# TensorE signals twice an expert tile instead of four times

## The chip, the cores and the metric

The kernel runs on one core of a Trainium2 chip. The metric is the device time of one execution in microseconds (us), the median over several runs.

## The reference

128 graphs of 128 nodes with 128 features go through a graph attention layer and then a mixture of experts, both with a layer norm ahead and a residual behind. The change touches the experts alone:

```python
logits = einsum('bsd,de->bse', x, gate_w) + gate_b        # 16384 tokens, 16 experts
top_probs, top_idx = top_k(softmax(logits), 2)            # two experts a token, gates normalized to 1
h1 = einsum('bsd,edh->bseh', x, w1)                       # 128 -> 256
h2 = einsum('bsd,edh->bseh', x, w2)                       # 128 -> 256
hidden = silu(h1) * h2
expert_out = einsum('bseh,eho->bseo', hidden, w3)         # 256 -> 128
out = x + einsum('bseo,bse->bso', expert_out, dispatch)
```

All data is float32.

## The kernel before

The attention part comes first, in 32 groups of four graphs. As each group's rows are ready, GpSimd scatters them into `first_list`, an array in device memory that is sorted by the token's first expert. When the list stands, the experts work through it in tiles of 256 rows (two times 128). Each tile's result is added to its rows, and GpSimd scatters these into `second_list`, sorted by the token's second expert (line 632). The second pass does the same over that list and scatters the rows to the output (line 643). A list has 72 tiles: 48 whole (one expert), 8 lone and 16 mixed (two experts, 128 rows each), so there are 144 tiles in all. `r` is the list, `j` the tile, `u` the tile's buffer of `S` = 12, and `n` the turn over these buffers. A part of each list's whole tiles runs in a loop on the engines (`Fori`), and the rest is written out.

The program has no scheduler. Each engine has a program of its own, and `done(engine, semaphores, n, u, d)` makes it wait until the step of tile `u + d` has been signalled; the semaphores of a kind stand in a list of `TURNS` = 4, taken in turn. For a tile `j` the engines do this:

- SyncE loads the rows to `xin` (lines 442 and 446) and copies the expert's first weights within the core to `we` (line 436), up to 12 tiles ahead.
- VectorE normalizes the rows, in the first list alone (line 989, named `xn`).
- TensorE, in `tile` from line 1248, does in this order: the gate product of tile j into `psG`, signal `s_G`; the up product into `psU`, signal `s_U` (both line 1258, four matmuls of 256 columns in a whole tile, and each shows as two in the profile); the two transposes of tile j + 2 into `psX` (line 1273), signal `s_xTp`; the second product of tile j - 1 into `psY` (line 1283), signal `s_Y`. A signal is an increment on the last matmul of its group.
- ScalarE, in `tile` from line 732: silu of the gate product (line 736, waits for `s_G`), then the copy of the transposed rows of tile j + 2 from `psX` to `xT` (line 741, waits for `s_xTp` and for `s_U`). The profile names `xT` and the hidden tile `hid` by the array `X` in which they lie, and the gate and up products by `psS`.
- VectorE: the product of silu and up product, `hid` (line 1083, waits for `s_U` and silu), then the normalization of a later tile, then the gated sum of tile j - 1 into `xin` (line 1092, waits for `s_Y`).
- GpSimd: every second tile it issues four scatters, two for each of the two tiles before (lines 632 and 643), when VectorE's sum is signalled.

TensorE in turn waits for `xT` and silu of two tiles before ahead of the gate product, for `hid` of two tiles before ahead of the up product, for the rows and `xn` ahead of the transposes, and for `hid` of the tile before ahead of the second product.

Of the kernel before, what the change touches and what calls it, by code (L numbers as in the profile page):

```python
# [5 lines left out]
def gnn_then_moe(nc: bass.Bass, x, adj, a0, a1, a2, a3, gate_w, gate_b, w1, w2, w3, out):  # L6
# [37 lines left out]
    S = 12  # L44
    SURE = (TOKENS - E * (W2 - 1)) // W2
    PAIRS = TOKENS // W2 - SURE
    TILES = SURE + E // 2 + PAIRS
# [31 lines left out]
    with ctx:  # L79
# [6 lines left out]
        def sem(name):  # L86
            return ctx.enter_context(nc.semaphore(name))
# [115 lines left out]
        TURNS = 4  # L203
# [9 lines left out]
        psG = [psS[:, 0, :], psS[:, 1, :]]  # L213
        psU = [psS[:, 2, :], psS[:, 3, :]]
# [72 lines left out]
        s_in = [sem(f"s_in{i}") for i in range(S)]  # L287
        s_we = [sem(f"s_we{i}") for i in range(S)]
        s_xn = [sem(f"s_xn{i}") for i in range(TURNS)]
        s_xTp = [sem(f"s_xTp{i}") for i in range(TURNS)]  # L290
        s_xT = [sem(f"s_xT{i}") for i in range(TURNS)]
        s_G = [sem(f"s_G{i}") for i in range(TURNS)]
        s_U = [sem(f"s_U{i}") for i in range(TURNS)]
        s_silu = [sem(f"s_silu{i}") for i in range(TURNS)]
        s_hid = [sem(f"s_hid{i}") for i in range(TURNS)]
        s_Y = [sem(f"s_Y{i}") for i in range(TURNS)]
# [11 lines left out]
        def wait(eng, s, value):  # L308

            if not isinstance(value, int) or value > 0:  # L310
                eng.wait_ge(s, value)
# [21 lines left out]
        LEAD, LAG = 2, 1  # L333
# [9 lines left out]
        def offsets(i, after):  # L343

            if i is None:
                return [after(S)[0] - S]
            return [k - i for k in after(i) if k < TILES]
# [19 lines left out]
        def wait_in(eng, n, u, d):  # L367

            wait(eng, s_in[(u + d) % S], (n + (u + d) // S + 1) * 32)

        def done(eng, sems, n, u, d):

            wait(eng, sems[(u + d) % TURNS], n * (S // TURNS) + (u + d) // TURNS + 1)
# [283 lines left out]
        def _(act):  # L657
# [65 lines left out]
            def closing():  # L723
                new_rows_turned(G - 2)
                new_rows_turned(G - 1)
                second_gate(G // 2 - 2)
                second_gate(G // 2 - 1)

            steps(step)
            closing()  # L730

            def tile(n, u, i, on):
                if on(0):
                    done(act, s_hid, n, u, -2)
                    done(act, s_G, n, u, 0)
                    nc.scalar.activation(silu[:, u % 2, :], psG[u % 2], ACT.Silu).then_inc(s_silu[u % TURNS], 1)  # L736
                for d in offsets(i, turned_after):
                    k = (u + d) % S
                    done(act, s_U, n, u, d - XTS)
                    done(act, s_xTp, n, u, d)  # L740
                    nc.scalar.activation(xT[:, k % XTS, :], psX[k % 2][:, 0:W2], ACT.Copy).then_inc(s_xT[k % TURNS], 1)  # L741

            def pad(r, rows, width, e):
# [359 lines left out]
        def _(pe):  # L1103
# [144 lines left out]
            def tile(r, n, u, i, weights, experts, between=None):  # L1248


                if weights:
                    done(pe, s_xT, n, u, 0)
                    parts = weights()
                    for half, out, s_out, s_free in ((0, psG[u % 2], s_G, s_silu), (1, psU[u % 2], s_U, s_hid)):
                        done(pe, s_free, n, u, -2)
                        for at, rows in parts:
                            for c in range(HC):
                                last = mm(out[:, c * W2 + rows.start:c * W2 + rows.stop],  # L1258
                                          at[:, half * H + c * P:half * H + (c + 1) * P], xT[:, u % XTS, rows],
                                          start=True, stop=True)  # L1260
                        last.then_inc(s_out[u % TURNS], 1)
                if between:
                    between()
                if experts:
                    e = experts()
                for d in offsets(i, turned_after):
                    k = (u + d) % S
                    done(pe, s_xT, n, u, d - 2)
                    if r == 0:
                        done(pe, s_xn, n, u, d)  # L1270
                    wait_in(pe, n, u, d)
                    for t in range(2):
                        last = nc.tensor.transpose(psX[k % 2][:, t * P:(t + 1) * P], xin[:, k, t, ROW:ROW2],  # L1273
                                                   ident[:, :])
                    last.then_inc(s_xTp[k % TURNS], 1)
                if experts:
                    k = (u - LAG) % S
                    done(pe, s_y, n, u, -LAG - 2)
                    done(pe, s_hid, n, u, -LAG)
                    for t in range(2):  # L1280
                        for c in range(HC):
                            at = c * W2 + t * P
                            last = mm(psY[k % 2][:, t * D:(t + 1) * D], hid[:, k % HIDS, at:at + P],  # L1283
                                      wts[:, ds(e[t] * EW + (UP + c * D), D)],
                                      start=(c == 0), stop=(c == HC - 1))
                    last.then_inc(s_Y[k % TURNS], 1)
# [47 lines left out]
```

## Time and profile before

| | us |
|---|---|
| median of 3 runs | 867.44 |
| lowest and highest | 866.37 and 876.10 |
| the profiled execution | 875.39 |
| its span, first to last instruction | 873.6 |
| mean granted TensorE clock | 0.937 |

The rows come from one profiled execution, so sums are made against 875.39. Busy time of TensorE is the union of matmuls, whose ends are modelled; PEld is the weight load of the same engine, which runs beside the matmuls. "Idle before" is the time in which the engine did nothing ahead of an instruction, with what ended it: another engine's instruction, "issue" (nothing that the profile shows) or "remote" (no instruction of this core that ended just then). In the timeline, consecutive instructions of a line are merged, with their count at the end.

### The profile page before, as it was taken

The numbers are of one execution on the slowest core, as the hardware profiler recorded it, in microseconds if no ns is written. First come the engines' busy times: TensorE is split into PE (matmuls) and PEld (weight loads), VectorE is DVE, ScalarE is ACT, GpSimd is POOL, SyncE is SP. The second block draws the span as 40 slices with busy tenths as digits, with TensorE's granted clock in tenths as the row PEclk, the third lists the DMA queues.
The fourth block names the chain that finished last, engine by engine and source line by source line (L and its number), as shares of the span: only waits on it lengthen the run. The fifth ranks groups of instructions, "written<-read, shape, count | busy, mean of one in ns | idle before, by whom it ended". The sixth has DMA issues, their size and how long they took to land.

```text
span 873.6 us, 17532 instructions
## 1 busy us (share of the span) xinstructions
PE 739.4 (85%) x4422; PEld 595.1 (68%) x4423; DVE 503.5 (58%) x1706; ACT 415.4 (48%) x1011; POOL 516.7 (59%) x670
## 2 busy tenths in 40 slices
PE   3899999999999766888988888987898888878895
PEld 2465656565666645677878777886787777777785
DVE  3799999999999863545454544543333233233332
ACT  7999999999999221222222222222222222222221
POOL 3337777778787765554645455554555645545555
PEclk9999999999999767999989988998999999999998
DMA  5233544332321144766666555634766565666640
GB/s 157 73 109 115 157 129 147 96 105 81 105 90 35 33 148 156 216 220 190 225 213 197 171 184 168 197 126 131 232 212 190 178 211 179 197 200 198 189 131 8
DMA packets 127462, 133.28 MB, mean 153 GB/s; under 512 B 16362, under 2 KB 98545, under 8 KB 127378
## 3 DMA queue, kind: packets, MB, share of 16 engines
q1 hardware_dynamic: 107008, 94.66, 36.0%
q0 software_dynamic: 15616, 34.38, 11.6%
q10 hardware_dynamic: 4754, 3.25, 1.2%
q8 instruction: 36, 0.59, 0.3%
q14 instruction: 48, 0.39, 0.2%
HBM read 52.28 MB, written 41.19 MB: 107 GB/s over the span
## 4 chain that ended last, share of the span: by engine, by line
PE 43%; DVE 23%; issue 16%; another core or an unknown queue 12%; ACT 4%; POOL 1%; DMA 0%; DVEq 0%; ACTq 0%; POOLq 0%
PE psS L1258 23%; PE bank L1283 13%; DVE stage L886 3%; PE bank L1273 3%; DVE stats L817 3%; DVE late L933 3%; DVE bestix L909 2%; DVE late L949 2%; DVE X L1083 1%; PE psS L1166 1%; ACT silu L736 1%; DVE late L968 1%; DVE best L905 1%; ACT late L689 1%
## 5 line engine op out<-in xcount | busy, mean ns | idle before, releaser
L1258 PE MATMUL psS<-X,late 128*128 128x256 f32 (+1 forms) x1280 | 264.1, 355 | 6.0 <-issue 5.8
L1258 PEld LDWEIGHTS psS<-X,late 128*128 128x128 f32 x1280 | 212.7, 203 | 26.0 <-issue 7.1
L1083 DVE TENSOR_TENSOR X<-silu,psS 128x512 f32<-128x512 f32 x144 | 98.8, 686 | 226.2 <-remote 119.8
L736 ACT ACTIVATE silu<-psS 128x512 f32<-128x512 f32 x144 | 86.0, 597 | 282.3 <-remote 147.2
L632 POOL DMA_INDIRECT second_list<-xin x144 | 142.2, 988 | 129.7 <-DVE xin L1092 88.7
L643 POOL DMA_INDIRECT out_dram<-xin x144 | 141.7, 984 | 122.4 <-DVE xin L1092 82.7
L1283 PE MATMUL bank<-wts,X 128*128 (+1 forms) x1152 | 168.1, 292 | 36.5 <-DVE X L1083 33.5
L1283 PEld LDWEIGHTS bank<-wts,X 128*128 128x128 f32 x1152 | 150.6, 203 | 45.9 <-issue 45.8
L583 POOL DMA_INDIRECT first_list<-stage,slot x128 | 128.1, 1001 | 52.6 <-issue 41.2
L1092 DVE SCALAR_TENSOR_TENSOR xin<-bank,xin 128x128 f32<-128x128 f32 x288 | 87.5, 346 | 100.7 <-remote 62.3
L1166 PE MATMUL psS<-late,hT 128*128 128x512 f32 x256 | 118.7, 607 | 3.0 <-ACT late L689 2.8
L741 ACT ACTIVATE X<-bank 128x256 f32<-128x256 f32 x144 | 55.2, 384 | 130.2 <-remote 69.1
L1273 PE MATMUL bank<-ident,xin 128*128 128x128 f32 x288 | 59.0, 289 | 40.6 <-issue 37.2
L1166 PEld LDWEIGHTS psS<-late,hT 128*128 128x128 f32 x256 | 47.1, 195 | 50.4 <-issue 47.5
L933 DVE TENSOR_REDUCE late<-psS 128x512 f32<-128x2048 f32 x32 | 72.9, 2279 | 12.9 <-PE psS L1171 12.8
L1273 PEld LDWEIGHTS bank<-ident,xin 128*128 128x128 f32 x288 | 39.7, 150 | 58.2 <-issue 50.3
L689 ACT ACTIVATE late<-bank,acol 128x512 f32<-128x512 f32 x128 | 77.6, 705 | 0.0
L565 POOL TENSOR_TENSOR norm<-veps,minus_half 128x8 f32<-128x8 f32 (+1 forms) x37 | 56.5, 1526 | 0.0
L718 ACT ACTIVATE h<-X,norm 128x128 f32<-128x128 f32 x128 | 53.4, 517 | 1.1 <-POOL norm L569 1.1
L697 ACT ACTIVATE late<-late,negmax 128x128 f32<-128x128 f32 x128 | 50.4, 427 | 6.5 <-DVE negmax L956 6.5
L989 DVE TENSOR_SCALAR xin<-xin 128x128 f32<-128x128 f32 x144 | 44.9, 359 | 0.0
L679 ACT ACTIVATE late<-late,shift 128x512 bf16<-128x512 int32 x64 | 43.3, 742 | 0.0
(156 smaller groups left out, 826.0 us busy)
## 6 DMA issues: line engine op xcount, KB each, us to landing
late<-wts SPq DMA_DIRECT2D x160, 256.0 KB
xin<-second_list SPq DMA_DIRECT2D x48, 262.0 KB
X<-in_x_dram SPq DMA_DIRECT2D x32, 256.0 KB
late<-in_adj_dram SPq DMA_DIRECT2D x32, 256.0 KB
xin<-first_list SPq DMA_DIRECT2D x48, 134.0 KB
xin<-second_list SPq DMA_DIRECT2D x48, 131.0 KB
wts<-in_L_ffn_w_dram SPq DMA_DIRECT2D x48, 128.0 KB
xin<-first_list SPq DMA_DIRECT2D x48, 67.0 KB
```

The source lines that it names most:

```text
L583: pool.indirect_dma_start(first_list[:, :], bass.IndirectOffsetOnAxis(ap=slot[:, g % SB, t:t + 1], axis=0), stage_v(g % SB)[:, t, :], None ...
L632: pool.indirect_dma_start(second_list[:, :], bass.IndirectOffsetOnAxis(ap=xin[:, at, k, SLOT1:SLOT1 + 1].bitcast(i32), axis=0), xin[:, at, ...
L643: pool.indirect_dma_start(out_rows[:, :], bass.IndirectOffsetOnAxis(ap=xin[:, at, k, DEST:DEST + 1].bitcast(i32), axis=0), xin[:, at, k, 0 ...
L689: last = nc.scalar.activation(hTa[s % 2][:, k, :], psT[:, :], ACT.Copy, scale=acol[:, k:k + 1])
L736: nc.scalar.activation(silu[:, u % 2, :], psG[u % 2], ACT.Silu).then_inc(s_silu[u % TURNS], 1)
L933: v.tensor_reduce(score.rearrange("p (t d) -> p t d", t=T), psS[:, :, :].rearrange("p t (k d) -> p t d k", k=K), AX, ALU.max).then_inc(s_s ...
L1083: v.tensor_tensor(hid[:, u % HIDS, :], silu[:, u % 2, :], psU[u % 2], ALU.mult).then_inc(s_hid[u % TURNS], 1)
L1092: last = v.scalar_tensor_tensor(at, psY[k % 2][:, t * D:(t + 1) * D], xin[:, k, t, GATE[r]:GATE[r] + 1], at, ALU.mult, ALU.add)
L1166: mm(psS[:, t, :], hT[:, g % 2, t * D:(t + 1) * D], hTa[g % 2][:, :, t * D:(t + 1) * D], start=True, stop=False)
L1258: last = mm(out[:, c * W2 + rows.start:c * W2 + rows.stop], at[:, half * H + c * P:half * H + (c + 1) * P], xT[:, u % XTS, rows], start=Tr ...
L1273: last = nc.tensor.transpose(psX[k % 2][:, t * P:(t + 1) * P], xin[:, k, t, ROW:ROW2], ident[:, :])
L1283: last = mm(psY[k % 2][:, t * D:(t + 1) * D], hid[:, k % HIDS, at:at + P], wts[:, ds(e[t] * EW + (UP + c * D), D)], start=(c == 0), stop=( ...
```

## The change

The gate product and, from the second tile of a list on, the transposes carry no signal any more. ScalarE's silu waits for the signal behind the up product. Its copy of the transposed rows of tile j + 2 waits for the signal behind the second product of tile j - 1, which TensorE does right after the transposes. Where a tile has no second product before it (the first two calls of each list), the transposes still signal, three a list, on one semaphore `s_xTp` that counts through. The order of the instructions on the engines stays as it is; lines behind the diff's second piece move by eight or nine (736 becomes 744, 741 becomes 749, 1258 becomes 1266, 1273 becomes 1281, 1283 becomes 1292).

```diff
--- before.py
+++ after.py
@@ -287,9 +287,8 @@
         s_in = [sem(f"s_in{i}") for i in range(S)]
         s_we = [sem(f"s_we{i}") for i in range(S)]
         s_xn = [sem(f"s_xn{i}") for i in range(TURNS)]
-        s_xTp = [sem(f"s_xTp{i}") for i in range(TURNS)]
+        s_xTp = sem("s_xTp")
         s_xT = [sem(f"s_xT{i}") for i in range(TURNS)]
-        s_G = [sem(f"s_G{i}") for i in range(TURNS)]
         s_U = [sem(f"s_U{i}") for i in range(TURNS)]
         s_silu = [sem(f"s_silu{i}") for i in range(TURNS)]
         s_hid = [sem(f"s_hid{i}") for i in range(TURNS)]
@@ -729,15 +728,24 @@
             steps(step)
             closing()
 
+            def turned(n, u, i, d):
+
+
+                if i is None or i > 0:
+                    done(act, s_Y, n, u, -LAG)
+                else:
+                    k = n * S + u + d
+                    act.wait_ge(s_xTp, k // TILES * (LEAD + 1) + k % TILES + 1)
+
             def tile(n, u, i, on):
                 if on(0):
                     done(act, s_hid, n, u, -2)
-                    done(act, s_G, n, u, 0)
+                    done(act, s_U, n, u, 0)
                     nc.scalar.activation(silu[:, u % 2, :], psG[u % 2], ACT.Silu).then_inc(s_silu[u % TURNS], 1)
                 for d in offsets(i, turned_after):
                     k = (u + d) % S
                     done(act, s_U, n, u, d - XTS)
-                    done(act, s_xTp, n, u, d)
+                    turned(n, u, i, d)
                     nc.scalar.activation(xT[:, k % XTS, :], psX[k % 2][:, 0:W2], ACT.Copy).then_inc(s_xT[k % TURNS], 1)
 
             def pad(r, rows, width, e):
@@ -1251,14 +1259,14 @@
                 if weights:
                     done(pe, s_xT, n, u, 0)
                     parts = weights()
-                    for half, out, s_out, s_free in ((0, psG[u % 2], s_G, s_silu), (1, psU[u % 2], s_U, s_hid)):
+                    for half, out, s_free in ((0, psG[u % 2], s_silu), (1, psU[u % 2], s_hid)):
                         done(pe, s_free, n, u, -2)
                         for at, rows in parts:
                             for c in range(HC):
                                 last = mm(out[:, c * W2 + rows.start:c * W2 + rows.stop],
                                           at[:, half * H + c * P:half * H + (c + 1) * P], xT[:, u % XTS, rows],
                                           start=True, stop=True)
-                        last.then_inc(s_out[u % TURNS], 1)
+                    last.then_inc(s_U[u % TURNS], 1)
                 if between:
                     between()
                 if experts:
@@ -1272,7 +1280,8 @@
                     for t in range(2):
                         last = nc.tensor.transpose(psX[k % 2][:, t * P:(t + 1) * P], xin[:, k, t, ROW:ROW2],
                                                    ident[:, :])
-                    last.then_inc(s_xTp[k % TURNS], 1)
+                    if not experts:
+                        last.then_inc(s_xTp, 1)
                 if experts:
                     k = (u - LAG) % S
                     done(pe, s_y, n, u, -LAG - 2)
```

What moves is what each instruction waits for. On ScalarE, in the second written-out turn of the first list, the rows stood so before (each row with the semaphores that it waits for):

```order
L736 ACTIVATE silu<-psS 128x512 [waits s_G2,s_hid0]
L741 ACTIVATE X<-bank 128x256 [waits s_xTp0,s_U2]
L736 ACTIVATE silu<-psS 128x512 [waits s_G3,s_hid1]
L741 ACTIVATE X<-bank 128x256 [waits s_xTp1,s_U3]
L736 ACTIVATE silu<-psS 128x512 [waits s_G0,s_hid2]
L741 ACTIVATE X<-bank 128x256 [waits s_xTp2,s_U0]
```

and stand so now, with `s_U` in place of `s_G` and `s_Y` in place of `s_xTp`:

```order
L744 ACTIVATE silu<-psS 128x512 [waits s_U2,s_hid0]
L749 ACTIVATE X<-bank 128x256 [waits s_Y1,s_U2]
L744 ACTIVATE silu<-psS 128x512 [waits s_U3,s_hid1]
L749 ACTIVATE X<-bank 128x256 [waits s_Y2,s_U3]
L744 ACTIVATE silu<-psS 128x512 [waits s_U0,s_hid2]
L749 ACTIVATE X<-bank 128x256 [waits s_Y3,s_U0]
```

Silu now waits for the up product's semaphore of its own tile, and the copy for the second product's.

## Rows read from the trace of the kernel before

**Rows 1.** The page: busy time by engine, then three of its groups by line
```profile
PE 739.4 (85%) x4422; PEld 595.1 (68%) x4423; DVE 503.5 (58%) x1706; ACT 415.4 (48%) x1011; POOL 516.7 (59%) x670
...
L736 ACT ACTIVATE silu<-psS 128x512 f32<-128x512 f32 x144 | 86.0, 597 | 282.3 <-remote 147.2
...
L643 POOL DMA_INDIRECT out_dram<-xin x144 | 141.7, 984 | 122.4 <-DVE xin L1092 82.7
...
L741 ACT ACTIVATE X<-bank 128x256 f32<-128x256 f32 x144 | 55.2, 384 | 130.2 <-remote 69.1
```

**Rows 2.** Windows, the expert part: length, busy (count) by engine, clock, DMA share
```profile
345.00:868.00 523.00, 446.23 (x2904) 402.69 (x2903) 210.30 (x557) 129.26 (x278) 276.67 (x281) 0.94 0.59 184
```

**Rows 3.** Groups by line, 345 to 868 us: weight loads of line 1258
```profile
L1258 PEld LDWEIGHTS psS<-X,late 128*128 128x128 f32 x1243 | 203.7, 201 | 22.2 <-issue 5.3
```

**Rows 4.** Waits, from 350 us: who waited for whom, us, times, longest
```profile
ACT silu L736 <- remote: 140.3, 34, 6.7
DVE X L1083 <- remote: 111.0, 22, 6.9
...
PE bank L1283 <- DVE X L1083: 33.5, 17, 4.8
...
PE bank L1273 <- issue: 28.0, 18, 3.7
```

**Rows 5.** Timeline, two tiles: start, length, engine, line, operation, count, idle before
```profile
640.14 1.06 PE L1283 MATMUL bank<-wts,X 128*128 x8
...
640.92 1.60 PEld L1258 LDWEIGHTS psS<-X,late 128*128 128x128 f32 x8
641.03 1.89 PE L1258 MATMUL psS<-X,late 128*128 128x256 f32 x8
642.01 0.98 POOL L643 DMA_INDIRECT out_dram<-xin  x1 [0.30 <-issue]
...
642.55 0.36 PEld L1273 LDWEIGHTS bank<-ident,xin 128*128 128x128 f32 x2
...
642.98 1.06 PE L1283 MATMUL bank<-wts,X 128*128 x8
...
643.87 1.89 PE L1258 MATMUL psS<-X,late 128*128 128x256 f32 x8
643.97 0.61 DVE L1092 SCALAR_TENSOR_TENSOR xin<-bank,xin 128x128 f32<-128x128 f32 x2 [3.10 <-remote]
...
644.11 0.60 ACT L736 ACTIVATE silu<-psS 128x512 f32<-128x512 f32 x1 [3.32 <-remote]
...
645.97 1.15 PE L1283 MATMUL bank<-wts,X 128*128 x8
```

**Rows 6.** Timeline, two tiles later, the same columns
```profile
646.96 1.89 PE L1258 MATMUL psS<-X,late 128*128 128x256 f32 x8
...
649.14 0.60 ACT L736 ACTIVATE silu<-psS 128x512 f32<-128x512 f32 x1 [2.67 <-PE psS L1258]
...
651.82 0.98 POOL L643 DMA_INDIRECT out_dram<-xin  x1 [0.30 <-issue]
652.75 0.69 DVE L1083 TENSOR_TENSOR X<-silu,psS 128x512 f32<-128x512 f32 x1 [4.98 <-remote]
...
653.89 1.21 PE L1283 MATMUL bank<-wts,X 128*128 x8 [1.97 <-DVE X L1083]
654.28 0.38 ACT L741 ACTIVATE X<-bank 128x256 f32<-128x256 f32 x1 [4.55 <-remote]
```

**Rows 7.** Timeline, a tile of the first list, the same columns
```profile
361.74 0.59 PE L1258 MATMUL psS<-X,late 128*128 128x256 f32 x2
...
364.15 0.60 ACT L736 ACTIVATE silu<-psS 128x512 f32<-128x512 f32 x1 [4.24 <-remote]
...
367.13 0.69 DVE L1083 TENSOR_TENSOR X<-silu,psS 128x512 f32<-128x512 f32 x1 [5.88 <-remote]
...
368.43 0.41 PE L1273 MATMUL bank<-ident,xin 128*128 128x128 f32 x2 [3.26 <-issue]
```

## The prediction

> **What bounds the kernel now.** I read the page's busy line first, then the window of the expert part, the groups by line, the waits and last the timeline of single tiles. TensorE is busy 85% of the span [rows 1]. In the expert stretch, 345 to 868 us, it is busy 446.2 of 523.0 us at a granted clock of 0.94, and no other engine comes near [rows 2]. So TensorE bounds the expert part, and its 76.8 idle us (523.0 - 446.2) are all that the change could win apart from matmul time. The change touches nothing ahead of the expert part.
>
> What is a tile worth undisturbed? In the timeline one tile's eight gate and up matmuls begin at 641.03 and the next tile's at 643.87: 2.84 us a tile [rows 5]. ScalarE does 278 operations in the stretch, two a tile [rows 2], so the mean is 523/139 = 3.76 us, 0.92 us more.
>
> Where is TensorE idle? The waits name two large entries: 33.5 us in 17 waits of the second product for VectorE's hidden tile (DVE X, line 1083) and 28.0 us in 18 waits before the transposes that the view lists as "issue" [rows 4]. Together 61.5 us in 35 stalls, 1.8 us each. The same view shows ScalarE's silu waiting 140.3 us and VectorE's product 111.0 us for "remote": for something that no instruction's end explains [rows 4]. The timeline explains it. In [rows 5] the tile's gate product is through at about 641.9 (half of the 1.89 us from 641.03), but its silu starts at 644.11, and at 643.97 VectorE begins on the output of a product that was through at 641.20 (640.14 + 1.06). Both engines begin within 0.14 us of each other, 2.8 and 2.2 us late: TensorE's signals had been held, and came out together. In [rows 6] one signal is let through at 649.14 (silu), one more at 652.75 (the product), and those behind at 654.28. In [rows 7] silu starts at 364.15, the product of the same tile only at 367.13, though the up product was done at 362.33 (its last two matmuls start at 361.74 and take 0.59). Each time GpSimd is issuing scatters, a row of 0.98 us every 1.29 us, and the last signals come out 0.9 to 1.5 us after the last scatter of the batch (642.99 to 643.97, 652.80 to 654.28) [rows 5, 6]. So TensorE is held up by its own late signals: VectorE gets them late, and TensorE then waits for VectorE.
>
> **The change, part by part.**
>
> *Two signals fewer on TensorE.* 144 gate signals and 144 transpose signals go, one for each silu and each copy [rows 1], but for 3 transposes a list that keep theirs: 282. Does a signal cost TensorE time of its own? The weight loads of 640.92 run eight in 1.60 us, end at 642.52, and the next group starts at 642.55, right across a gate signal in the middle and an up signal at the end [rows 5]. The mean weight load is 201 ns over all of them [rows 3]. A signal costs at most those 0.03 us, and the same step is there without one. I take 0; the bound is -282 x 0.03 = -8.5 us.
>
> The Trainium skill (TensorE: Matmul & The Clock Gate, "The cost: per-tile semaphore tail") says that increments of matmuls serialize, each some 26 ns of tail; by it 282 increments would be 7.4 us, an estimate from that page. This trace does not show that time between the weight loads, so the sum does without it.
>
> *Silu waits for the up product.* It starts four matmuls later: 1.89/2 = 0.9 us. With signals in time nothing waits for it. The tile whose up product ends at 642.92 (641.03 + 1.89) has its second product at 645.97, 3.05 us later, and silu (0.60) and product (0.69) need 1.29 us of that [rows 5]. Cost 0, with 1.8 us of cover.
>
> *The transposed copy waits for the second product.* That is 1.06 us later at most, the second product's own length, which ends at 644.04 (642.98 + 1.06) [rows 5]. The copy is used by the gate product of the tile at 646.96, and takes 0.38 us, so 2.5 us of cover remain [rows 5, 6]. Behind it in ScalarE's queue stands the next silu, whose own signal comes with the end of the next up product, 1.7 us after, so the queue is not moved. Cost 0. While TensorE stands at the second product, the copy stands too, but the gate product behind it reads the copy of one tile before.
>
> *Fewer signals in the held queue.* This is the term that decides, and it has two signs. Take the stalls of [rows 6] and [rows 7]. Just ahead of the silu at 649.14 one signal was let through, the gate's. The up signal was ready: the eight matmuls from 646.96 end at 648.85. It was not let through until 652.7, and TensorE stalled 1.97 us. In the changed kernel the up signal stands where the gate's stood. If it gets that turn, silu and product are done by 650.5 (649.14 + 0.60 + 0.69 and two handovers) and the whole stall goes. In [rows 7] likewise: with the up signal at 364.15 the product would start at 364.8 and the transposes, which now start 1.30 us after it (368.43 - 367.13), at 366.1 and not at 368.43. If it does not get the turn and comes out with the rest at 652.7 or 367.1, silu, which was already done before, is now ahead of the product, and the stall is longer by 0.60 us and a handover: 0.65 us. Where gate and up signal come out together at the end, as at 644.1 in [rows 5], nothing changes.
>
> So each of the 35 stalls is worth between -1.8 us (mean length, gone) and +0.65 us. All gone would be -61.5 us, all longer +22.8 us; these are the ends. The rows show early turns in two of three episodes, and in one of those a second turn before the end. But a turn seems to depend on the scatters, so not every one falls where an up signal stands first. I take 4 in 10 stalls won: 35 x (0.4 x -1.8 + 0.6 x 0.65) = 35 x -0.33 = -12 us.
>
> *Against it, GpSimd.* It issues 144 scatters a list [rows 1]; four, with their gaps, take 4 x 1.29 = 5.2 us of each two tiles, and two undisturbed tiles last 5.7 us [rows 5]. When stalls go, the batches move closer together, so that a larger share of the time is held. That caps the gain, one reason for 0.4 and not more.
>
> *Clock.* 0.06 of 523 us, 31 us at most, is lost to the granted clock [rows 2]. I take no part of it.
>
> *Sum.* The profiled execution took 875.39 us (span 873.6, and 1.8 around it). 875.4 - 12 = 863. The median of the runs shown is 867.44, 8.0 below the profiled one, so on the scale of the medians 867.4 - 12 = 855.
>
> **The rivals.**
>
> *Every signal is served by itself (834 us).* If a held path takes a time for each signal, whatever stands there, half the signals mean nearly half the holding. In [rows 6] the gate, up and transpose signals each come out at a time of their own (649.1, 652.7, 654.3), which speaks for it. Against it, 643.97 and 644.11 in [rows 5] come out in one rush. Then about half of the 61.5 us go, and some clock with them: -33, 834 us.
>
> *The holding is a window that no count of signals changes (867 us).* Signals are let out when the scatters' batch has landed. Then wins and losses are few and cancel: 867. The rush at the end in [rows 5] speaks for it, the single turns against.
>
> *Silu takes the gate's head start away (888 us).* The mechanism sits at the second product, where TensorE waits for VectorE. The price is 0.65 us for every stall that ends with the up signal. It decides if the up signal, whose place in the queue is the gate's, wins fewer than a quarter of the turns (0.65/(1.8 + 0.65) = 0.27 is where gain and loss cancel). With turns won in none of the 35, the price is 22.8 us, less some stalls in which gate and up signal come out together: +20 us, 888. For it speaks that silu had its signal first in both [rows 6] and [rows 7]; against it that something has to get the turn that the gate had.
>
> *TensorE's own pace (859 us).* If a signal does cost the 0.03 us of the step between groups, 282 of them give -8.5 us where TensorE is the bound: 859. The equal steps in [rows 5] speak against it. By the skill's tail rule named above it would be much the same time.
>
> *The change does not do what it says.* ScalarE's waits are replaced one for one, and three transposes a list still signal, so it does; a wait left on a counter that is reached anyway costs nothing.
>
> **How the numbers follow.** Turn taken in part (855): 0.45. Each signal by itself (834): 0.22. Window (867): 0.15. Silu's head start (888): 0.13. TensorE's pace (859): 0.05. The middle case runs from 846 (half the stalls won and a few us of clock) to 866 (three in ten). The range for 8 in 10 goes from 830, just under the per-signal case, to 876, past the window case and part of the loss. A measurement of this kernel can tell about 2%, 17 us, from no change: under 850 is faster, over 885 slower. Faster: 0.22 and a quarter of the middle case, 0.33. Slower: most of the loss case, 0.11. Within: 0.56.
>
> **What would show it.** In the changed kernel's waits, the second product's waits for VectorE and the "issue" ones before the transposes should sum to some 50 us in place of 61.5, in fewer waits. ScalarE's silu should follow the up product's end and never the gate's; "remote" waits should be shorter where a turn was won. Weight loads should step as before; if the mean of 201 ns falls, TensorE's pace was the thing. If the number of stalls stays and each is about 0.6 us longer, silu's head start was worth more than the turns. If busy time of the expert stretch stays near 446 us and idle drops to 45 us or less, each signal is served by itself. The forecast is wrong if the stalls vanish altogether, or if new ones appear before the gate product for the transposed copy, which would mean that its 2.5 us of cover was not there.

## The result: 0.8% slower

| | before | changed |
|---|---|---|
| median of 20 runs | 870.12 us | 877.06 us |
| lowest and highest | 866.37 and 876.10 | 873.36 and 886.46 |
| the profiled execution | 875.39 | 875.26 |
| its span | 873.6 | 873.5 |

The ratio is 1.0081, with a 95% interval of 1.006 to 1.0101. The forecast was 855 us, faster. The kernel is slower by 7 us, which is small and yet clear of noise. The median of before over these 20 runs is 2.7 us above the 867.44 from which the forecast started. Both profiled executions took the same time: that of before stands at the upper end of its runs, that of the changed kernel near the lower end of its own. So the profiles show where the waits went, but not the 7 us themselves.

The waits of the changed kernel from 345 us on, the counterparts of [rows 4] (line 744 is silu, 749 the copy, 1266 the gate and up product, 1281 the transposes, 1292 the second product, 1091 VectorE's product):

```profile
DVE X L1091 <- ACT silu L744: 158.6, 72, 6.6
ACT silu L744 <- remote: 97.7, 21, 6.2
...
PE bank L1292 <- DVE X L1091: 31.2, 12, 4.0
...
PE bank L1281 <- issue: 15.8, 15, 3.6
...
DVE X L1091 <- remote: 13.4, 4, 3.8
...
PE bank L1281 <- DVE xin L997: 10.0, 5, 3.2
PE psS L1266 <- ACT X L749: 8.1, 12, 1.5
...
PE psS L1266 <- issue: 2.6, 4, 1.0
```

Three lines of the kernel before that [rows 4] does not show:

```profile
DVE X L1083 <- ACT silu L736: 57.6, 53, 6.2
...
PE psS L1258 <- issue: 8.1, 14, 1.2
...
PE bank L1273 <- DVE xin L989: 3.3, 1, 3.3
```

The window and the weight loads that answer to [rows 2] and [rows 3]:

```profile
345.00:868.00 523.00, 450.80 (x2907) 404.22 (x2906) 209.07 (x563) 129.33 (x278) 277.98 (x282) 0.94 0.58 183
```

```profile
L1266 PEld LDWEIGHTS psS<-X,late 128*128 128x128 f32 x1246 | 204.2, 202 | 25.6 <-ACT X L749 6.6 <-issue 1.5
```

VectorE's product now waits 158.6 us for silu, where it was 57.6 us, and 13.4 us for "remote", where it was 111.0. Together that is 172.0 us for 168.6: most of this wait has only changed its name, because silu now stands between the late signal and the product. TensorE waits 31.2 us for the hidden tile, where it was 33.5; the two entries before the transposes are 15.8 and 10.0 us, where one had 28.0 and the other 3.3. A new one of 8.1 us in 12 waits stands ahead of the gate product, for the copy, and the "issue" entry there went from 8.1 to 2.6 us. In the window TensorE is idle 72.2 us (523.0 - 450.8), where it was 76.8, and busy 4.6 us more. The weight load takes 202 ns in the mean, where it took 201. TensorE's signals are held as before: silu still waits 97.7 us for "remote".

A stretch of the changed kernel's timeline (start, length, engine, line, operation, count, idle before) shows one such episode:

```profile
644.70 1.89 PE L1266 MATMUL psS<-X,late 128*128 128x256 f32 x8
...
645.68 0.38 ACT L749 ACTIVATE X<-bank 128x256 f32<-128x256 f32 x1 [1.30 <-PE bank L1292]
...
647.54 1.89 PE L1266 MATMUL psS<-X,late 128*128 128x256 f32 x8
...
648.95 0.98 POOL L642 DMA_INDIRECT out_dram<-xin  x1 [0.30 <-issue]
...
651.63 0.60 ACT L744 ACTIVATE silu<-psS 128x512 f32<-128x512 f32 x1 [5.56 <-remote]
...
652.12 0.38 ACT L749 ACTIVATE X<-bank 128x256 f32<-128x256 f32 x1
652.36 0.69 DVE L1091 TENSOR_TENSOR X<-silu,psS 128x512 f32<-128x512 f32 x1 [6.12 <-ACT silu L744]
...
653.65 1.23 PE L1292 MATMUL bank<-wts,X 128*128 x8 [4.00 <-DVE X L1091]
```

The up product of the tile from 644.70 is through at 646.59. Its silu starts at 651.63, 5 us late, 1.7 us after the last scatter ended at 649.93. Only then can VectorE's product follow, at 652.36, and TensorE resumes at 653.65. In [rows 6] silu had been done when the up signal came out, and the product started right with it. That is the head start that the change gives away. In this episode the up signal got no turn at the start of the held stretch.

The traces also record when an increment became visible, for some four in five of TensorE's signals. These records bear out the reading of [rows 6]: the tile's gate signal is visible at 648.76, its up signal at 652.37, 3.8 us after the matmul's end, and the next five in a rush from 653.90 to 654.18. In the changed kernel's episode the up signal becomes visible at 651.25 and the next two 0.1 us apart behind it. ScalarE's and VectorE's own increments are visible 8 to 11 ns after the end in the median, so only TensorE's are held among these three.

### The profile page after: what moved, and what is told of

Same layout as the page of the kernel before. It is cut to its first block, busy times and chain, and to the rows that moved or that the text cites. A ratio compares the mean times of both kernels' runs of the same rounds, so it can differ in the third digit from the quotient of the medians.

```text
span 873.5 us, 17532 instructions
## 1 busy us (share of the span) xinstructions
PE 743.0 (85%) x4422; PEld 596.0 (68%) x4423; DVE 501.4 (57%) x1706; ACT 415.4 (48%) x1011; POOL 516.7 (59%) x670
## 4 chain that ended last, share of the span: by engine, by line
PE 40%; DVE 23%; issue 15%; another core or an unknown queue 13%; ACT 7%; POOL 1%; ACTq 0%; DMA 0%; DVEq 0%; POOLq 0%
PE psS L1266 23%; PE bank L1292 12%; DVE late L941 4%; DVE stage L894 3%; DVE stats L825 3%; PE bank L1281 3%; ACT silu L744 2%; DVE bestix L917 2%; DVE late L957 2%; DVE X L1091 1%; ACT late L688 1%; ACT X L749 1%; DVE best L913 1%; DVE late L976 1%
## 5 line engine op out<-in xcount | busy, mean ns | idle before, releaser
L1266 PE MATMUL psS<-X,late 128*128 128x256 f32 (+1 forms) x1280 | 267.5, 359 | 11.4 <-issue 6.2
L1292 PE MATMUL bank<-wts,X 128*128 (+1 forms) x1152 | 166.4, 290 | 33.8 <-DVE X L1091 31.2
L1292 PEld LDWEIGHTS bank<-wts,X 128*128 128x128 f32 x1152 | 148.7, 201 | 43.1 <-issue 42.5
L1100 DVE SCALAR_TENSOR_TENSOR xin<-bank,xin 128x128 f32<-128x128 f32 x288 | 87.3, 345 | 71.9 <-remote 48.4
L1281 PE MATMUL bank<-ident,xin 128*128 128x128 f32 x288 | 58.7, 288 | 31.2 <-issue 21.1
```

The source lines that it names most:

```text
L1100: last = v.scalar_tensor_tensor(at, psY[k % 2][:, t * D:(t + 1) * D], xin[:, k, t, GATE[r]:GATE[r] + 1], at, ALU.mult, ALU.add)
L1266: last = mm(out[:, c * W2 + rows.start:c * W2 + rows.stop], at[:, half * H + c * P:half * H + (c + 1) * P], xT[:, u % XTS, rows], start=Tr ...
```

## The experiments

### One signal at a time, and signals that nobody waits for

These four ran on one chip with the kernel before, at 863.74 us.

**Gate signal kept, transposes' signal dropped** (against the changed kernel):

```diff
-                    done(act, s_U, n, u, 0)
+                    done(act, s_G, n, u, 0)
...
-                    last.then_inc(s_U[u % TURNS], 1)
+                        last.then_inc(s_out[u % TURNS], 1)
```

> The gate signal is back, and silu waits for it as before; only the transposes' signal is gone and the copy waits for the second product. Theory A (what costs is that the copy waits for the second product: in the changed kernel TensorE stalls 8.1 us in 12 waits ahead of the gate product for the copy): as slow as the changed kernel, 1.006 to 1.012 of before, with those 12 waits there. Theory B (what costs is that silu waits for the up product, 0.65 us more in each stall that ends with the up signal): no slower than before, 0.99 to 1.00, and VectorE waits for silu no longer than the 57.6 us of before. Both theories have dropped signals help a little.

Measured: 862.09 us, 0.9983 of before (0.9952 to 1.0014). Its waits:

```profile
DVE X L1092 <- remote: 109.2, 25, 5.6
...
DVE X L1092 <- ACT silu L745: 48.4, 54, 6.1
...
PE bank L1293 <- DVE X L1092: 28.3, 13, 3.4
...
PE psS L1267 <- ACT X L750: 5.8, 9, 1.3
```

The waits for the copy are there, 9 with 5.8 us, and cost no time that can be measured. Theory A falls. VectorE waits for silu 48.4 us, as little as before, and for "remote" 109.2 us.

**Gate signal dropped, transposes' signal kept** (against the kernel before):

```diff
-                    done(act, s_G, n, u, 0)
+                    done(act, s_U, n, u, 0)
...
-                        last.then_inc(s_out[u % TURNS], 1)
+                    last.then_inc(s_U[u % TURNS], 1)
```

> The transposes' signal is back, and the copy waits for it as before; only the gate signal is gone and silu waits for the up product. Theory A: no slower than before, 0.99 to 1.00, and no waits for the copy ahead of the gate product. Theory B: as slow as the changed kernel, 1.006 to 1.012, with TensorE's stalls for the hidden tile near 0.6 us longer each.

Measured: 874.83 us, 1.013 (1.0096 to 1.0164). The whole loss sits in this half of the change.

```profile
DVE X L1082 <- ACT silu L735: 173.4, 75, 7.4
...
PE bank L1282 <- DVE X L1082: 32.9, 17, 4.2
...
PE bank L1272 <- issue: 17.2, 11, 3.8
...
DVE X L1082 <- remote: 12.7, 3, 5.0
```

VectorE's wait for silu is 173.4 us. But TensorE's stalls for the hidden tile are not 0.6 us longer each: 32.9 us in 17 waits are those of [rows 4], and against the run with the gate signal kept, on the same chip, they are more in number (13 there) and not longer (28.3 us). That part of theory B's expectation missed. The profiles of these two runs are 8.7 us apart (866.96 and 875.68). From 345 us to the end TensorE is idle 75.8 us with the gate signal and 82.1 us without; its waits for the hidden tile grow by 4.6 us, and the other entries move by 1 to 3 us either way. Another 2.4 us are busy time, at a mean granted clock of 0.948 and 0.936. With one profile of each kernel this is a picture and not a measurement.

**The changed kernel's waits, four signals sent:**

```diff
-                    last.then_inc(s_U[u % TURNS], 1)
+                        last.then_inc(s_U[u % TURNS] if half else s_idle, 1)
...
-                    if not experts:
-                        last.then_inc(s_xTp, 1)
+                    last.then_inc(s_idle2 if experts else s_xTp, 1)
```

> The waits of the changed kernel with four signals a tile: the gate and transpose groups increment semaphores that nobody waits for. If a signal in the held queue takes a time of its own (the reason for which I forecast a gain), this is slower than the changed kernel by more than 10 us, 1.02 of before or above. If the signals' number is worth nothing and the later waits alone made the 0.8%, it is equal to the changed kernel, 1.006 to 1.010.

Measured: 874.44 us, 1.0118 (1.008 to 1.0157). That is just above the expected 1.006 to 1.010 and overlaps with the changed kernel's 1.006 to 1.0101, which was measured in another set of runs; on this chip the run with the gate signal dropped had 1.013. The two signals that the change takes away are worth at most a few tenths of a per cent, and the later waits alone make the loss.

**The kernel before with eight signals a tile:**

```diff
+                                if c == 0 and at is parts[0][0]:
+                                    last.then_inc(s_more[half], 1)
...
+                        if t == 0:
+                            last.then_inc(s_more[2], 1)
...
+                        if t == 0:
+                            last.then_inc(s_more[3], 1)
```

> The kernel before with eight signals a tile in place of four; the four more go to semaphores that nobody waits for. If each signal takes a time of its own in the held queue, the delays add up and it is slower by 20 us or more (1.02 and above). If the queue is let out by the scatters' progress however many signals stand in it, no more than 2 us (1.00). If a signal costs TensorE 0.03 us of its own pace, 4 x 144 x 0.03 = 17 us (1.02) with the same stalls and longer steps between weight loads.

Measured: 863.83 us, 1.0023 (1.0001 to 1.0045). Four more signals on each of 144 tiles cost 0.2%, some 2 us for 576 signals: 3.5 ns each, and 7 ns at the interval's end. The mean weight load of the whole program is 202 ns, where the page of before had 203:

```profile
L1259 PEld LDWEIGHTS psS<-X,late 128*128 128x128 f32 x1280 | 211.5, 202 | 19.6 <-issue 1.0
```

So neither the held queue nor TensorE's own pace depends measurably on the number of signals, and the reason for which I forecast a gain is gone.

The recorded increments show the same at the up signal itself. This is how late it became visible after the end of its matmul, from 345 us on, in one profile of each kernel (some 138 up signals each, the rest not recorded):

| | recorded | mean lateness | over 0.5 us late |
|---|---|---|---|
| before | 114 | 1.56 us | 57% |
| gate signal kept, transposes' dropped | 101 | 1.58 us | 65% |
| before, eight signals | 120 | 1.48 us | 62% |
| changed | 111 | 1.25 us | 59% |
| gate signal dropped | 115 | 1.28 us | 53% |
| changed, four signals sent | 113 | 1.24 us | 58% |

The standard error of a mean is 0.13 to 0.16 us. Where silu waits for the up signal, that signal comes some 0.3 us less late, but it does so with the gate signal sent as well as without, so it is not a turn won by a missing signal. Why it does, no run shows. It is less than the 0.60 us of silu and the handover, 0.65 us, that now stand between the signal and the product: the product can start up to some 0.35 us later in the mean.

### More cover for the hidden tile

The next four ran on another chip, with the kernel before at 871.03 us. First, the second product two tiles behind the first ones, before and changed:

```diff
-        LEAD, LAG = 2, 1
+        LEAD, LAG = 2, 2
-        HIDS, XTS = 2, 2
+        HIDS, XTS = 3, 2
```

and for the changed kernel `turned` takes the second product from the third tile on.

> The kernel before (all four signals and its waits) with the second product two tiles behind the first ones in place of one, and three hidden tiles. Theory B (held signals reach VectorE late, and TensorE then stands at the second product): the second product's 33.5 us of waits for the hidden tile shrink to under 10, and as the up product of two tiles on still waits for the same hidden tile, some 10 us of the gain are kept, 0.985 to 0.995 of before. Rival (the stalls are held up elsewhere, in the chain from signals through VectorE to the rows of the next tiles): the waits only move to the transposes or the up product, 0.995 to 1.005.

> The same depth with the changed kernel's two signals and waits. Theory B: the 0.65 us that silu's later start costs lies in the added cover, so the time is within 0.3% of the run with depth two and four signals. Rival (silu's head start is lost in the chain through VectorE, whose queue holds the hidden tile, the normalization and the sum in one order, wherever TensorE stands): it is slower than that run by the same 0.8 to 1.2% as without the depth.

Measured: four signals 875.14 us, 1.0051 (1.002 to 1.0082); two signals 879.68 us, 1.0112 (1.0078 to 1.0147). The waits with four signals, from 350 to 870 us:

```profile
DVE X L1083 <- ACT silu L736: 25.4, 38, 6.0
...
PE psS L1258 <- ACT X L741: 14.7, 8, 2.6
...
PE bank L1283 <- issue: 10.2, 16, 1.1
```

and with two signals:

```profile
DVE X L1091 <- ACT silu L744: 187.5, 74, 9.1
...
PE psS L1266 <- ACT X L749: 25.4, 21, 3.3
...
PE bank L1292 <- issue: 7.7, 12, 1.1
```

The second product's wait for the hidden tile is gone from both, and nothing was gained. TensorE now stands ahead of the gate product for the copy, 14.7 us in 8 waits with four signals and 25.4 us in 21 with two, and its waits of all kinds with four signals add up to 75.7 us, where those of before are 75.4. The rival of the first expectation was right in kind, at the edge of its range; the second result, 0.6%, lies between theory B's 0.3% and the rival's 0.8 to 1.2%. My picture of the place was too narrow. It is not one wait that costs, but the chain behind a held signal. How the chain does it is an argument from the order of the queues, which no run takes apart. ScalarE's queue has silu ahead of the copy, and VectorE's has the product ahead of the normalization and the sum. With the gate signal, silu has often run when the rest comes out, and the copy can go at once. Without it, silu's 0.60 us stands before both. The difference of the two kernels, 0.6%, is near the 0.8% without the depth.

### What holds the signals

In the second list GpSimd's scatters are left out; ScalarE issues plain DMAs to fixed rows, so most of the output isn't written. SyncE's waits follow these DMAs' semaphores.

```diff
+            def tile_out(n, u, i, on):
+                tile(n, u, i, on)
+                if on(-2):
+                    done(act, s_y, n, u, -2)
+                    at = (u - 2) % S
+                    for k in range(2):
+                        act.dma_start(out_rows[(2 * at + k) * P:(2 * at + k + 1) * P, :],
+                                      xin[:, at, k, 0:D]).then_inc(s_zp[at], 16)
...
-            for r, out_of in ((0, first_out), (1, second_out)):
+            for r, out_of in ((0, first_out),):
```

> The kernel before, but in the second list GpSimd's scatters are left out: ScalarE issues two plain hardware DMAs a tile of the same rows to fixed rows of the output (so most of the output isn't written). If the scatters hold TensorE's signals, then in the second list silu starts right behind the gate product, remote waits of silu and of VectorE's product all but vanish there, TensorE's waits for the hidden tile too, and the time falls by 20 to 40 us (0.955 to 0.975). If SyncE's loads or anything else holds them, remote waits stay and the time with them (0.99 to 1.01).

> The same with the changed kernel's signals and waits. Theory B with scatters as the holder: with signals in time silu has 1.8 us of cover, so in the second list nothing is lost; against the plain rows with four signals half of the 0.8 to 1.2% is left, from the first list alone (1.003 to 1.006). If silu's later start costs without any holding, the whole difference is left.

Measured: four signals 817.00 us, 0.9384 (0.9343 to 0.9425); two signals 816.88 us, 0.9423 (0.9368 to 0.9479). The second list in the kernel before and then without scatters, each from its first silu to its last (length, then busy by PE, PEld, DVE, ACT and POOL, granted clock, DMA share, GB/s):

```profile
607.00:861.00 254.00, 219.39 (x1469) 200.19 (x1468) 87.77 (x211) 64.11 (x141) 135.78 (x139) 0.97 0.60 186
```

```profile
606.00:809.00 203.00, 200.72 (x1452) 188.37 (x1451) 91.62 (x211) 69.31 (x142) 0.00 (x0) 1.00 0.78 237
```

```profile
ACT silu L741 <- PE psS L1272: 98.3, 70, 1.8
DVE X L1097 <- PE psS L1272: 79.2, 67, 1.2
...
ACT silu L741 <- remote: 2.8, 1, 2.8
```

TensorE is busy 200.7 of 203.0 us, where it was 219.4 of 254.0: 32 us of the 51 were idle time, 19 us busy time. "Remote" is down to one wait of 2.8 us for silu, though the DMA share is higher, 0.78 for 0.60. In the same trace TensorE's gate and up signals are 1.3 and 1.4 us late in the mean in the first list, and 13 to 14 ns in the median in the second. So the scatters hold TensorE's signals, and without them in this list the whole kernel is 54 us shorter, more than the expected 20 to 40. SyncE's loads, which are all still there, don't. The edit swaps three things at once, the engine that issues, the indirect addressing and the rows that are written, and which of them holds the signals stays open.

Four runs of each form can't tell the expected 0.3 to 0.6% between two and four signals: both medians are 817 us, the ratios 0.4% apart, and their intervals overlap. The traces can, for the second list. From its first silu's start to its last one's it takes 202.6 us with four signals (606.1 to 808.7) and 202.1 us with two (603.7 to 805.8). Where nothing is held the two-signal form loses nothing.

**Other batches, an edit that changes nothing.** If a batch of scatters holds the signals, its size could matter. `BATCH` is 2 tiles before; these ran on a third chip, with before at 864.89 us.

```diff
-            BATCH = 2
+            BATCH = 1
```

> The kernel before with GpSimd's scatters issued after every tile, two at a time, in place of four every second tile. If TensorE's signals are held from about the second scatter of a batch until about 1 us after its last, a batch of two holds for a shorter time than half a batch of four: shorter stalls, 0.97 to 0.99 of before. If what counts is only how many scatters there are, 0.995 to 1.005.

> The same batches of two with the changed kernel's signals and waits. Theory B: shorter holding leaves more of silu's later start under cover, so it is slower than the batches of two with four signals by less than the 0.8% of before against changed, 0.2 to 0.6%. Rival (one more holding a tile, each of which can catch the up signal): the difference grows to over 1%.

and with `BATCH = 4` and four signals:

> The kernel before with eight scatters every fourth tile. If a batch holds TensorE's signals for its whole length, some 10 us, it outlasts the cover of a tile by far: TensorE stalls longer for the hidden tile, 1.02 to 1.06 of before. If only the number of scatters counts, 0.995 to 1.005.

Measured: 864.13 us, 0.9998 (0.9967 to 1.003); with two signals 871.64 us, 1.0073 (1.0042 to 1.0104); with `BATCH = 4` 865.55 us, 0.9982 (0.9944 to 1.002).

These runs say nothing on the size of a batch, because `BATCH` does not set it. GpSimd's program for the experts is a plain list: wait for the sum of a tile, issue its two scatters, wait for the next tile's sum. `BATCH` only moves the place in the source where that list is written out; with 1, 2 and 4 the same 144 waits and 288 scatters stand in the same order. The traces agree: from 345 us on the 284 scatters form 60 rows (gaps under 1.1 us) in the kernel before, 32 of four and 25 of six, and 58 rows each with `BATCH` 1 and 4. What makes rows is that the sums are signalled in rushes. So it is not right that GpSimd waits for every second tile to issue four, and both runs with four signals are repeats of the kernel before, 0.02% and 0.18% away from it. The run with two signals is a repeat of the change on another chip: 0.7% slower. Whether the size of a batch matters is not tested.

### Silu's length, and a chip on which nothing is held

To see whether the price is silu's own 0.60 us, silu was cut to 32 columns:

```diff
-                    nc.scalar.activation(silu[:, u % 2, :], psG[u % 2], ACT.Silu).then_inc(s_silu[u % TURNS], 1)
+                    w = HC * W2 if isinstance(n, int) and n == 0 and u < 2 else 32
+                    nc.scalar.activation(silu[:, u % 2, 0:w], psG[u % 2][:, 0:w], ACT.Silu).then_inc(s_silu[u % TURNS], 1)
```

> The kernel before with silu cut from 512 to 32 columns from the third tile on (the rest of the silu tile stays as an early tile left it, so the output is another). This is the control: with the gate signal silu mostly runs before the up signal comes out, so its length matters little, 0.990 to 1.000 of before.

> The gate signal dropped as in the second run, which was 1.3% slower than before, and silu cut to 32 columns. If the price is silu's length ahead of the product, about two thirds of it go (a 597 ns silu becomes some 200 ns): within 0.5% of the control with four signals. If the price is something else about the later wait, the difference to the control stays 1.0 to 1.6%.

> The changed kernel with silu cut to 32 columns. By silu's length: within 0.4% of the control. Otherwise 0.8 to 1.2% above the control, as the changed kernel is above the one before.

Measured: 741.11 us, 1.0008 (0.9986 to 1.0029); 741.86 us, 1.0015 (0.9993 to 1.0036); 743.59 us, 1.004 (1.0016 to 1.0065). The surprise is in none of these ratios: on this, a fourth chip, the kernel before itself took 740.28 us. A second set has the changed kernel beside:

> The changed kernel once more. Where the kernel before takes some 865 us, 1.006 to 1.011 of it. Where it takes some 740 us, so that signals come out in time, silu's later start lies under the cover: 1.000 to 1.004.

> The gate signal alone dropped. Where the kernel before takes some 865 us, 1.008 to 1.016; where it takes some 740 us, 0.998 to 1.003.

> The kernel before with silu cut from 512 to 32 columns from the third tile on, the control. Where the kernel before takes some 865 us: 0.985 to 1.000 of it, since with the gate signal silu mostly runs before the up signal comes out.

> The gate signal dropped and silu cut to 32 columns. Where the kernel before takes some 865 us: by silu's length ahead of the product, within 0.6% of the control, where the whole silu has 1.3%; if the price is something else about the later wait, 1.0 to 1.6% above the control.

It ran on the same chip, with before at 740.46 us. Measured: changed 741.68 us, 1.0015 (0.9989 to 1.0042); gate signal alone dropped 741.74 us, 1.001 (0.9987 to 1.0034); short silu 741.05 us, 0.9998 (0.9973 to 1.0022); short silu without the gate signal 742.64 us, 1.0023 (1.0 to 1.0047). The changed kernel's expert part on that chip, as window, waits and timeline:

```profile
320.00:735.00 415.00, 409.35 (x2925) 383.49 (x2924) 208.59 (x577) 137.92 (x282) 286.22 (x292) 0.99 0.75 235
```

```profile
DVE X L1091 <- ACT silu L744: 195.1, 135, 7.1
ACT silu L744 <- PE psS L1266: 192.1, 138, 3.0
ACT X L749 <- PE bank L1292: 71.7, 132, 3.6
```

```profile
600.71 0.98 POOL L642 DMA_INDIRECT out_dram<-xin  x1 [0.57 <-issue]
600.76 0.60 ACT L744 ACTIVATE silu<-psS 128x512 f32<-128x512 f32 x1 [1.29 <-PE psS L1266]
...
601.46 0.69 DVE L1091 TENSOR_TENSOR X<-silu,psS 128x512 f32<-128x512 f32 x1 [1.54 <-ACT silu L744]
...
601.67 1.89 PE L1266 MATMUL psS<-X,late 128*128 128x256 f32 x8
...
602.00 0.98 POOL L642 DMA_INDIRECT out_dram<-xin  x1 [0.30 <-issue]
...
603.66 0.60 ACT L744 ACTIVATE silu<-psS 128x512 f32<-128x512 f32 x1 [1.35 <-PE psS L1266]
```

TensorE is busy 409.4 of 415.0 us, and its waits from 330 us on add up to 6.7 us in 5 waits. GpSimd's scatters run on, at 600.71 and 602.00, and silu still starts at 603.66, 0.1 us after the up product's end at 603.56. All 132 up signals that this trace records from 345 us on are visible 14 or 15 ns after the end of their matmul. Here scatters hold nothing. Against the changed kernel of the first profile the expert part is 108 us shorter (415 for 523), 67 us of it idle time of TensorE and 41 us busy time, at a granted clock of 0.99 for 0.94.

Without held signals the change costs at most little: 0.15% for the changed kernel, 0.1% for the gate signal alone, both within noise. Of the five runs with silu behind the up product one lies clear of 1, the changed kernel with short silu, 1.004 (1.0016 to 1.0065), and all five lie above 1, so a cost of 0.1 to 0.4% is not excluded. What silu's length costs when signals are held was not measured: both sets ran on this chip.

## Why the prediction was wrong

- **TensorE bounds the expert part and is held up by its own late signals; scatters go with it.** Right. Without scatters the second list took 203 for 254 us, and the recorded increments show the lateness itself, 1.6 us in the mean at the up signal and up to 5.6 us.
- **A signal costs TensorE nothing.** Right: 576 more signals cost about 2 us, the term taken was 0. The rival on TensorE's own pace is out. The section of the Trainium skill that the prediction cites for 26 ns an increment (TensorE: Matmul & The Clock Gate, "The cost: per-tile semaphore tail") is about small matmuls packed side by side into the array, while these fill it; by its figure 576 increments would be some 15 us, an estimate, and the run's interval ends at 4 us.
- **Silu waits for the up product: 0 with signals in time.** Right where it was tested, to within a few tenths of a per cent on the chip without holding and by 202.1 for 202.6 us in the list without scatters.
- **The transposed copy: 0, with 2.5 us of cover.** The cost was right (0.9983 with that half alone). The cover was not: the waits that I had named as the sign of a mistake came, 12 with 8.1 us, because held signals are later than 2.5 us. They took the place of others.
- **Fewer signals in the held queue: -12 us.** This is the step that failed. I had read the single turns of [rows 6] as a queue in which one signal less moves the others forward, and gave the up signal the gate signal's turn in 4 of 10 stalls. The single turns are real, but the count of signals does not move them: sending the two dropped signals again changed nothing (1.0118 for 1.0081), four more cost 0.2%, and more than half of the up signals are over 0.5 us late whether two, four or eight are sent (59, 57 and 62%). The 0.3 us that the up signal gains in the mean it gains with all four sent too, and the term's other side, silu's 0.65 us between up signal and product, is larger. The two together measure +7 us, where I wrote -12. By my 0.65 us an episode that is as if 7/0.65 = 11 stalls had been lengthened and none won; the stalls themselves do not show it so (12 waits for the hidden tile with 31.2 us for 17 with 33.5).
- **GpSimd caps the gain.** I reasoned with batches that GpSimd issues every second tile. It has none: the rows of scatters follow the sums as they are signalled. No run tests the cap.
- **The signs that I named.** The one for my own case came: the waits for the hidden tile and the "issue" ones before the transposes sum to 47.0 us in 27, for 61.5 in 35, and silu's "remote" waits fell from 140.3 to 97.7 us. It did not mean a gain. With the waits for VectorE's rows and for the copy the sum is 65.1 us, for 64.8 before. The sign against it, new waits for the copy, was the one to heed.
- **The rivals.** The sign was that of "silu takes the head start away", which had 0.13, and dropping the gate signal alone gave 1.013 against 0.9983 for the other half. The net was a third of what I wrote, and its place was too narrow: with the second product's wait gone, the difference stays at 0.6%. "Every signal is served by itself", which had 0.22 and pulled the range down, is refuted. The window rival had it right that the count of signals changes nothing, and the sum wrong by those 7 us. The time lies 1 us above the range's end, and 2.7 us of its 22 us distance from 855 come from the median of three runs as the base. By the term's own formula three stalls in ten won would be 864 and not the 866 that the middle case ends at.

Open: the split between silu's own length and other effects of its later start; what in the scatters holds the signals, and whether their grouping matters; and why some chips hold them and one did not.

## What to carry to other kernels

Before counting signals, ask what hangs on each. A signal behind half of the work gives its reader a head start, and where signals arrive late in irregular stretches that head start is worth more than the trace's cover in a quiet tile suggests; sending it costs a few nanoseconds. Look at remote waits: here they pointed to a cost of some 50 us in one list that none of the signal arrangements tried here touched, and that leaving out GpSimd's scatters removed. Add up all waits of the bounding engine before and after, since single entries swap names. Check that an edit changes the instructions, and not only the source. And a kernel that is measured on one chip alone may be tuned against something that another chip does not do.

## What the runs showed of the hardware

While GpSimd's indirect scatters ran, TensorE's semaphore increments became visible late on the chips on which the kernel before took 864 to 871 us: in the kernel before 57% of the recorded up signals by more than 0.5 us, 1.6 us in the mean, 5.6 us at most. ScalarE's and VectorE's increments took 8 to 11 ns in the median in the same trace. With plain DMAs from ScalarE in place of the scatters TensorE's took 13 to 14 ns. On one chip the same program took 740 us, 15% less, with the same scatters; in the changed kernel's trace from there TensorE's up signals took 14 or 15 ns. An increment on a matmul cost about 3.5 ns (576 more in 2 us).
